# One copy for the g of two groups, one for the P x of two groups, and four exponentials ahead of the second group's transpose copy

## What is computed

```python
xn = (x - moving_mean) * rsqrt(moving_var + 0.001) * gamma + beta
q = xn @ Wq + bq;  k = xn @ Wk + bk;  v = xn @ Wv + bv
scores = einsum('bhid,bhjd->bhij', q, k) * 64 ** (-0.5)
attn = softmax(scores, axis=-1)
out = einsum('bhij,bhjd->bhid', attn, v) @ Wo + bo
return xn + out
```

## Time and profile before

| | |
|---|---|
| median of 3 runs | 4721.29 us |
| time of the profiled execution | 4727.12 us |
| its span, first to last instruction | 4724.9 us |
| granted TensorE clock, mean | 0.998 of full speed |
| steps, pairs of steps | 512, 256 |
| busy: PE, POOL, DVE, ACT | 96%, 95%, 95%, 91% |
| busy share of the DMA engines (queue 1) | 85.3% |

### The profile page before, as it was taken

How to read it: one execution, slowest core, us unless ns; L and a number is a source line. 1 busy time by engine, 2 the same in 40 slices (tenths; PEclk the granted TensorE clock), 3 DMA queues, 4 the chain that set the end, 5 groups by cost and what they waited for, 6 DMA issues and landing times.

```text
span 4724.9 us, 187136 instructions
## 1 busy us (share of the span) xinstructions
PE 4540.1 (96%) x59416; PEld 3778.9 (80%) x59416; DVE 4495.3 (95%) x7970; ACT 4297.6 (91%) x18437; POOL 4508.7 (95%) x2824
## 2 busy tenths in 40 slices
PE   7999999999999999999999999999999999999999
PEld 5888888888888888888888888888888888888887
DVE  7999999999999999999999999999999999999998
ACT  7999999999999999999999999999999999999998
POOL 7999999999999999999999999999999999999998
PEclk9999999999999999999999999999999999999999
DMA  7888888888888888888888888888888888888886
GB/s 141 174 173 172 173 172 172 172 173 172 173 171 172 172 172 172 172 173 173 171 173 173 172 173 171 172 172 172 172 172 172 173 171 172 173 172 173 171 173 139
DMA packets 4294236, 806.28 MB, mean 171 GB/s; under 512 B 4294208, under 2 KB 4294208, under 8 KB 4294208
## 3 DMA queue, kind: packets, MB, share of 16 engines
q1 hardware_dynamic: 4293312, 805.80, 85.3%
q10 hardware_dynamic: 896, 0.13, 0.0%
HBM read 537.10 MB, written 268.44 MB: 170 GB/s over the span
## 4 chain that ended last, share of the span: by engine, by line
ACT 36%; DVE 26%; PE 20%; issue 15%; DVEq 2%; POOL 1%; DMA 0%; ACTq 0%; POOLq 0%
ACT probs L335 29%; PE uo_ps L643 10%; DVE xT L559 7%; PE score_ps L624 6%; ACT probsT L351 5%; DVE row_stat L530 5%; DVE uo_ps L455 4%; DVE probsT L549 3%; DVE row_stat L490 3%; ACT g L360 3%; PE tg_ps L670 3%; DVE attn L446 2%; DVE neg_top L501 1%; DVE inv_sum L473 1%; PE tg_ps L682 1%
## 5 line engine op out<-in xcount | busy, mean ns | idle before, releaser
L335 ACT ACTIVATE probs<-score_ps,neg_top 128x128 f32<-128x128 f32 x8192 | 2890.5, 384 | 301.9 <-DVE neg_top L501 301.9
L277 POOL TENSOR_TENSOR x_weighted<-x_in,row_weights 128x1024 f32<-128x1024 f32 x1024 | 2402.7, 2371 | 21.8 <-DVE x_weighted L433 21.8
L335 ACT ACTIVATION_READ_ACCUMULATOR probs<-score_ps,neg_top 128x1 f32 x8192 | 1835.5, 224 | 0.0
L624 PE MATMUL score_ps<-xT,g 64*128 64x128 f32 x16384 | 1165.3, 281 | 152.3 <-ACT probs L335 152.3
L624 PEld LDWEIGHTS score_ps<-xT,g 64*128 64x128 f32 x16384 | 1015.1, 188 | 236.9 <-issue 235.4
L288 POOL TENSOR_TENSOR x_scaled_rows<-x_weighted,out_bias 128x512 f32<-128x512 f32 x1024 | 1199.9, 1199 | 0.0
L692 PEld LDWEIGHTS uo_ps<-w_o,uT 128*128 128x128 f32 x8192 | 994.9, 192 | 244.0 <-issue 243.7
L299 POOL TENSOR_TENSOR y<-attn,x_scaled_rows 128x512 f32<-128x512 f32 x768 | 982.3, 1279 | 190.8 <-DVE attn L446 190.8
L682 PE MATMUL tg_ps<-xT,w_g 128*128 128x512 f32 x2048 | 1019.2, 620 | 4.7 <-DVE xT L559 3.5
L643 PE MATMUL uo_ps<-probsT,x_in 128*64 128x128 f32 x16384 | 1008.5, 276 | 0.0
L692 PE MATMUL uo_ps<-w_o,uT 128*128 128x128 f32 x8192 | 997.4, 275 | 0.0
(11 more groups left out here) (70 smaller groups left out, 2019.1 us busy)
## 6 DMA issues: line engine op xcount, KB each, us to landing
x_quads<-in_x SPq DMA_DIRECT2D x4096, 64.0 KB, 2.2
x_in<-in_x SPq DMA_DIRECT2D x1024, 256.0 KB, 3.2
out<-y SPq DMA_DIRECT2D x1024, 256.0 KB, 2.4
norm_row<-in_L_conv_gamma ACTq DMA_DIRECT2D x1, 32.0 KB, 2.1
norm_row<-in_L_conv_beta ACTq DMA_DIRECT2D x1, 32.0 KB, 3.7
norm_row<-in_L_conv_bo SPq DMA_DIRECT2D x1, 32.0 KB, 3.4
norm_row<-in_L_conv_moving_mean ACTq DMA_DIRECT2D x1, 32.0 KB, 3.3
norm_row<-in_L_conv_moving_var ACTq DMA_DIRECT2D x1, 32.0 KB, 4.6
```

Of the source, the lines that this page charges most:

```text
L277: nc.gpsimd.tensor_tensor(x_weighted[:, n % 4, :, 0:2 * C].rearrange("p s (h c) -> p s h c", h=2), x_in[:, n % 8, :, None, :].broadcast_to ...
L335: last = nc.scalar.activation(probs[:, n % 4, q, :], score_ps[n % 2][:, q // PAIRS, q % PAIRS * W:(q % PAIRS + 1) * W], ACT.Exp, bias=neg_ ...
L624: last = nc.tensor.matmul(score_ps[n % 2][:, h, k * W:(k + 1) * W], g[half, s, k, :], xT[half, n % 8, k, :], start=True, stop=True)
```

## The change

`keep_g` is called once for each pair of groups and copies both halves of `tg_ps`, 1024 columns, in one instruction; it waits for both projections. `keep_u` is called once for each pair and copies both parts of a `uo_ps` that is now one tile over two banks; it waits for both P x. PE's waits for `g_kept` and `u_kept` now name the second group of the pair, also where only the first is used. On ACT, four exponentials instead of two stand ahead of the copy of the second group's transposes, and the first two exponentials of group 2t+1 stand ahead of the g copy.

```diff
-        uo_ps = [psum(f"uo_ps{i}") for i in range(2)]
+        uo_both = psum("uo_ps", (128, 2, 512))
+        uo_ps = [uo_both[:, i] for i in range(2)]
...
             def keep_g(r, n, peeled):
...
+                act.wait_ge(g_made[parts(n - 1)], uses(r, n - 1))
                 act.wait_ge(g_made[s], uses(r, n))
                 if exists(r, n - 4, peeled):
+                    act.wait_ge(scores_made[parts(n - 5)], uses(r, n - 5))
                     act.wait_ge(scores_made[s], uses(r, n - 4))
-                nc.scalar.activation(g[:, s].rearrange("p k w -> p (k w)"), tg_ps[:, n % 2],
+                nc.scalar.activation(g[:, s - 1:s + 1].rearrange("p n k w -> p (n k w)"), tg_ps[:].rearrange("p n x -> p (n x)"),
                                      ACT.Identity, bias=g_bias[:, 0:1]).then_inc(g_kept[s], 1)
 
             def step(r, t, peeled):
                 keep_probsT(r, 2 * t - 2, peeled)
-                exponentials(r, 2 * t, peeled, range(0, 2))
+                exponentials(r, 2 * t, peeled, range(0, 4))
                 keep_probsT(r, 2 * t - 1, peeled)
-                exponentials(r, 2 * t, peeled, range(2, 8))
-                keep_g(r, 2 * t + 2, peeled)
+                exponentials(r, 2 * t, peeled, range(4, 8))
+                exponentials(r, 2 * t + 1, peeled, range(0, 2))
                 keep_g(r, 2 * t + 3, peeled)
-                exponentials(r, 2 * t + 1, peeled, range(0, 8))
+                exponentials(r, 2 * t + 1, peeled, range(2, 8))
...
             def keep_u(r, n, peeled):
...
+                dve.wait_ge(u_made[parts(n - 1)], uses(r, n - 1))
                 dve.wait_ge(u_made[s], uses(r, n))
                 if exists(r, n - 2, peeled):
+                    dve.wait_ge(o_made[parts(n - 3)], uses(r, n - 3))
                     dve.wait_ge(o_made[parts(n - 2)], uses(r, n - 2))
-                nc.vector.tensor_copy(uT[:, n % 2], uo_ps[n % 2][:].rearrange("p (k w) -> p k w", k=PAIRS)) \
+                nc.vector.tensor_copy(uT[:].rearrange("p n k w -> p (n k w)"), uo_both[:].rearrange("p n x -> p (n x)")) \
                     .then_inc(u_kept[s], 1)
...
                 find_max(r, 2 * t + 1, peeled)
-                keep_u(r, 2 * t - 4, peeled)
                 keep_u(r, 2 * t - 3, peeled)
...
-                    pe.wait_ge(g_kept[s], uses(r, n))
+                    pe.wait_ge(g_kept[parts(n | 1)], uses(r, n | 1))
...
-                        pe.wait_ge(g_kept[parts(n + 2)], uses(r, n + 2))
                         pe.wait_ge(g_kept[parts(n + 3)], uses(r, n + 3))
...
-                    pe.wait_ge(u_kept[s], uses(r, n))
+                    pe.wait_ge(u_kept[parts(n | 1)], uses(r, n | 1))
```

More of the change, by code:

```diff
@@ L680, in project @@
                 elif exists(r, n - 2, peeled):
-                    pe.wait_ge(g_kept[parts(n - 2)], uses(r, n - 2))
+                    pe.wait_ge(g_kept[parts((n - 2) | 1)], uses(r, (n - 2) | 1))
                 nc.tensor.matmul(tg_ps[:, n % 2], w_g_all, xT[:, n % 8].rearrange("p k w -> p (k w)"),
```

## The result

The changed kernel takes 4877.27 us (median of 3 runs, 4875.42 to 4878.23), against 4721.29 us: 1.0328 times as long, 95% interval 1.0304 to 1.0351. That is 156 us more where 138 were forecast; it lies inside the range.

What follows compares the result with a forecast made beforehand. The bound was a ring of waits through PE, DVE and ACT, 18.28 us a pair. Changed: 3.70 + 0.04 + 1.13 + 6.16 + 7.79 = 18.82, +0.54 over 255 pairs, 138 us, giving 4859 us; range 4775 to 4915.

Steps and rivals of the forecast that it cites:

- The copy of P x in step A: DVE, the pair's step where the first copy ran beside PE's second P x: merged, 1.13 us follow instead of 0.61, +0.52.
- the ring: Waits around a pair of steps: PE scores to P x 3.70, DVE 6.81, ACT 7.77, together 18.28 us.
- The late projection: PE, behind four exponentials and the transpose copy: projection waits 0.86 us behind P x; ACT's g copy then waits 0.22.
- X_B: Start of ACT's exponentials in step B, the pair's other step; forecast 11.03 us after step A's exponentials end.
- E_B: End of ACT's exponentials in step B; forecast 9.0 us after step A's exponentials end.
- the half with slack: From the end of step A's exponentials through step B's own on ACT; taken as off the ring, some 1.5 us to spare.
- Q_A: End of PE's P x in step A, forecast 3.70 us after that step's exponentials; the merged copy may not start earlier.
- The saving on g: ACT: merged g copy 1.00 us instead of 1.19, -0.19 a step, only step B's on the ring; eaten by the projection.
- The tie of ACT and PE at the end of the ring: Before the second scores: ACT's sum gives a pair of 18.82 us, PE's own line from the projection 18.91.
- Fewer instructions win: Rival, chance 0.08: P x ends early enough for the merged copy, ring 0.24 shorter, -61 us, 4660.
- All near ties break: Rival, chance 0.07: output delayed, PE's restart costs over 0.14, copy 1.20; about 0.3 more a pair, +215 us, 4936.
- the two slower rivals: Projection's wait absent or covered (chance 0.20, +82 us, 4803), and all near ties break (0.07, +215 us, 4936).

Runs made afterwards that it cites:

- e1_one_u: The kernel before with the one merged copy of P x alone (one tile, merged waits): 4866.9 us, ratio 1.0300.
- e5_no_u: The changed kernel with two copies of P x as before, one copy of g and new ACT order kept: 4725.8 us, ratio 1.0002.
- e3_order: The kernel before with the new order of ACT's exponentials alone, two copies each of P x and g: 4716.7 us, ratio 0.9982.
- e8_g_twice: The changed kernel with two copies of g instead of one, all else as changed: 4869.0 us, ratio 1.0304.
- e6_g_ahead: The kernel before with one copy of g and two exponentials of group 2t+1 ahead of it, two copies of P x: 4677.8 us, ratio 0.9899.
- e4_two_ahead: The changed kernel with two instead of four exponentials ahead of the transpose copy: 4829.8 us, ratio 1.0221.
- e2_one_g: The kernel before with one copy of g alone, in its old place behind the eighth exponential of 2t: 4965.6 us, ratio 1.0509.

## Why the prediction was right

- **The copy of P x in step A**, forecast at +0.52 on the ring: the copy occupies 1.14 us instead of 0.61 and starts 0.10 instead of 0.04 behind P x, +0.59. e1_one_u shows that it makes the loss alone (+142 us, 145 by its expectation), e5_no_u that without it there is none. Three more pairs of kernels differ in it alone, and it costs 152 us in each: e3_order and e8_g_twice, e5_no_u and the change (151.5), e6_g_ahead and e4_two_ahead. Why it is 10 us more there than in e1_one_u is open.
- **The late projection**, forecast 0.86 behind P x with a cost of 0.2 a pair: it starts 0.55 behind P x (2410.24 to 2410.79). The restart itself is as forecast (2.57 behind X_B, summed 1.37 + 1.02 + 0.14 = 2.53); it is P x of step B that ends later: 4.06 behind E_B (2406.18 to 2410.24) instead of 3.70. What was off is the 3.70, read in step B of the kernel before and taken over as fixed: the last pair of scores waits for DVE's copy of a half of the transposes (L556), which stands in the list behind the late copy of P x. It ends at 2406.53 + 0.68 = 2407.21, and PE's weights for the last pair follow at 2407.32, as the rows below show. This delay lies in the half with slack, and a later P x only shortens the projection's own wait, so that it moved no time. The cost of the late projection was right in kind and near in size: 47 us against e4_two_ahead and 48 between e5_no_u and e6_g_ahead, summed 0.22 x 255 = 56.

```profile
2406.53 0.68 DVE L556 COPY probsT<-tg_ps 128x512 f32<-128x512 f32 x1
```

```profile
2407.32 0.33 PEld L630 LDWEIGHTS score_ps<-xT,g 64*128 64x128 f32 x4 [0.25 <-issue]
```

- **PE's output**, "nothing to pay, but nothing left over": it does wait for the merged copy, 0.3 us once a pair (72.0 us in 244 waits). This is in step A, behind Q_A, where the ring has gone over to DVE.
- **The saving on g**, forecast at 1.00 us for the merged copy and eaten in the ring: it occupies 1.02 (2412.83 to 2413.85), between my 1.00 and the 1.04 by the Trainium skill (ScalarE: Activation LUTs, on what ACT_TABLE_LOAD costs), whose 1133 ns for its duration compare with 1114 here. ACT waits 0.26 for the projection (2412.23 + 0.34 to 2412.83), forecast 0.22. That nothing of it reaches the time, e8_g_twice shows.
- **Waits.** The merged copy waits 0.82 us for PE in step A, forecast about 1, and 0.22 in step B, forecast hardly at all; the later P x of step B makes the second. In front of X_B 1.55 us, forecast about 1.5; for L515 0.24, forecast 0.4; the projection 134 us in total, forecast some 200.
- **The tie of ACT and PE at the end of the ring**, forecast within 0.05: ACT is at its end at 2416.05, 7.83 behind X_B; PE's line from the projection to the end of P x is 8.96, as the sum has it (18.82 + 3.70 - 13.56). Both are there at the same time.
- **The size.** +0.60 a pair where +0.54 was summed, 15 us of the 18 missing: the turn walked above, 18.92, is 0.10 above the sum, 0.06 by the start of the copy behind P x and 0.01 to 0.02 each by the copy's length, the four exponentials and the longer L352; the mean of the two stretches is 0.04 lower. Small terms, all to one side, on a ring that is walked 255 times.
- **The rivals.** "Fewer instructions win" fell: its condition, the copy ready by 2401.6, is not met. The rule of the Trainium skill behind it (Perfetto Trace Analysis, optimizing Scalar/DVE operations) does not hold here without a condition: the same merge of g costs 240 us in e2_one_g, where the copy waits for a later producer, and gains 47 in e6_g_ahead, where ready work covers that wait. For P x no run covers the wait. "All near ties break" came true at the output, off the ring, and with 0.04 us at g; its own 4936 us lies outside the range, though the text says that the range takes in most of the two slower rivals.

What my view of the kernel before lacked is the ring of e2_one_g, scores to projection to g to exponentials. I had called the half from E_A to E_B slack without adding up what a g copy that waits for both projections does there; in the change itself two exponentials cover it.

## What to carry to other kernels

Before two copies are merged, look at what each waits for: where the second one's input is the last to come, the first copy is hidden work, and merging moves its length behind that input. Pay for a merged copy with the wait that it needs: put work of the same engine that is ready, here two exponentials, in front of it, and see that this work does not push back what the copy waits for. A single engine's busy share tells neither; add up the ring of waits, each way around, and price an edit by what of it stands on the ring.

## What the runs showed that was not expected

Costs of single parts did not simply add up from the kernel before. The new order of ACT took 8 us off it (e3_order, 4716.7 against 4725.0), and the one copy of g, where two exponentials cover its wait, took 47 off (e6_g_ahead); both at once, in e5_no_u, give nothing (4725.8). Four exponentials ahead of the transpose copy make the projection late, the merged g copy has to wait for all of it, and the saving is gone. The copy of P x stands apart from this: it costs 152 us with either order and with one or two copies of g.

The copy of the transposes itself lasts 1.04 us behind four exponentials where it lasted 1.02 behind two, with the same operands. From its start to the start of the next exponential it is 0.91 and 0.90 (2409.61 to 2410.52, and the earlier trace rows), so what it occupies hardly grows; the record's length does.
